# Expert rows summed by accumulating DMAs into four arrays in memory, instead of by the engines after all of them have landed

## The chip, the core and the metric

The kernel runs on one core of a Trainium2 chip. The metric is the device time of one execution, in microseconds; smaller is better. The core has TensorE (PE; its weight loads are PEld), VectorE (DVE), ScalarE (ACT), GpSimd (POOL) and SyncE (SP), and 16 DMA engines that all of them share. In this kernel SP, ACT and POOL issue DMAs.

## What is computed

One transformer layer on 8 sequences of 256 tokens, width 256, all in float32: attention with 16 heads and a distance bias, a layer norm, then a mixture of 32 experts of which each token uses 6, plus a shared expert, and a second layer norm. The part that matters here:

```python
w, idx = _gate(xf, gate_w)                       # 6 of 32 experts per token
g = einsum('td,eid->tei', xf, w11)
u = einsum('td,eid->tei', xf, w33)
act = silu(g) * u
y = einsum('tei,te,edi->td', act, c, w22)        # c: the 6 weights of a token
shared = silu(xf @ sw1.T) * (xf @ sw3.T) @ sw2.T
x = layernorm(x + (y + shared))
```

So each of the 2048 tokens (16 tiles of 128) needs the sum of six rows of 256 floats, one from each of its experts, added to its row of x + shared.

## The kernel before

The program is written out by hand, one instruction stream per engine, with semaphores between them. It has four stages.

**Attention, routing (0 to 310 us).** Eight batches of 256 tokens (`BATCH`), one after the other (`attention_loop`), software-pipelined: while batch b is worked on, PE projects q and k of batch b+1 (`project_q`), ACT and DVE split them into two parts (q_hi, q_lo, k_hi, k_lo), and SP rearranges them through memory (`pack`): four stores to `q_scratch` and `k_scratch`, a wait until all four have landed, then four loads of `q_pack` and two of `k_pack` (L345, L348, L355, L360). PE's scores of batch b+1 (L494) stand in PE's order among the last work of batch b and wait for `qk_packed`. SP works its list in order: in `body(b)` it packs batch b+1, loads, and keeps the normed rows (`keep_x1`). In `body(1)` alone, behind these, it writes the padding rows of the array `routed` (`write_pads`, L383): 8 DMAs of 516 KB from the SBUF tile `empty`, in rows of 1032 bytes. Then comes the loop whose first body packs batch 3. POOL scatters each token's row six times into `routed`, an array in memory with a region for each expert (`dispatch`, L1307, 96 indirect DMAs of 128 rows). Each row carries in its column 256 a code that says where its result belongs, and in column 257 its weight.

**Expert weights and shared expert (310 to 372 us).** 24 DMAs of 512 KB load all expert weights into the SBUF tile `expert_w`.

**The slot loop (372 to 604 us).** The routed rows are worked in `SLOTS` = 128 slots of 128 rows of one expert each. Per slot: SP loads the rows (`xg`, L430), PE turns them (L674), multiplies with w11 and w33 (L682), ACT applies silu (L889), DVE works out the destination rows (`out_row`, L1239) and the product (L1242), PE turns it (L690) and multiplies with w22 (L698), ACT scales into a buffer `ey` (L895), of which there are eight, and POOL sends the 128 result rows of 1 KB with one indirect DMA (`send`, L1320) to `expert_out`, an array with six rows per token. Nothing but its own buffer's readiness (`ey_ready`) holds a send up.

**The last stage (604 to 665 us).** When all sends have landed, SP loads `expert_out` back, one tile of 128 tokens x 6 rows x 1 KB (768 KB) per DMA (`load_y`, L447), into the place of `expert_w`. The tiles are summed in pairs (`pair_loop`): the even tile of a pair by DVE (a reduction L1265 and an add L1270), the odd one by POOL (L1335) and PE (L736, L740, L743, sums in PSUM). Then statistics (L1272, L1276, L1279), an inverse root on ACT and DVE (`polish`), and two applications on ACT (L909), and a store of 256 KB (L913).

Of the kernel before, what the change touches and what calls it, by code (L numbers as in the profile page):

```python
# [50 lines left out]
F_STATS = 7  # L51
# [8 lines left out]
C_ID, C_TRI, C_IOTA, C_SLOT, C_PACK, C_END = 0, 128, 256, 288, 289, 321  # L60
# [46 lines left out]
def build(nc, xT, x, wq, wk, wv, wo, bias, consts, gate_w, expert_weights, sw1, sw3, sw2, out):  # L107
    ctx, early = ExitStack(), ExitStack()
    with ctx:
# [9 lines left out]
        def dram(name, shape, dt=F32):  # L119
# [7 lines left out]
        expert_out = dram("expert_out", [TOKENS * TOPK, DIM])  # L127
# [19 lines left out]
        codes = sb("codes", [P, TILES, TOPK], I32)  # L147
# [70 lines left out]
        expert_w = sb("expert_w", [P, TILES * TOPK * DIM], F32, late)  # L218
# [8 lines left out]
        rows_y = expert_w[:].rearrange("p (t n) -> p t n", t=TILES)  # L227
        f_out = [resid, x1[0]]
        f_resid = x1[1][:]
        y_sum = x1T[0][:, 0, :]  # L230
        y_half = [attn_T[i] for i in range(2)]
        f_bn = sb("f_bn", [P, 2, 2, 6])
        f_mv = sb("f_mv", [P, 2, 2, 2])
        f_small = sb("f_small", [P, 2, 8, 2])
# [39 lines left out]
        y_loaded = [sem(f"y_loaded{i}") for i in range(4)]  # L274
        f_paired = sem("f_paired")
        f_summed, f_stat, f_root, f_fin, f_done = (
            sem("f_summed"), sem("f_stat"), sem("f_root"), sem("f_fin"), sem("f_done"))
# [37 lines left out]

        def pair_loop(eng, body):

            body(0, 0, 0)
            with eng.Fori(0, (TILES // 2 - 2) // 2) as i:
                body(2 * i + 1, 1, i)  # L320
                body(2 * i + 2, 0, i + 1)
            body(TILES // 2 - 1, 1, TILES // 4 - 1)


        @block.sync
        def _(sp):
# [57 lines left out]

            def keep_x1(b, par):
# [4 lines left out]
            def body(b, par, h, one_behind, two_behind, ahead):  # L390
# [48 lines left out]
            for k in range(UNROLL):  # L439
                sp.wait_ge(ey_sent[k], 16 * SLOTS // UNROLL)  # L440
            y_view = expert_out.rearrange("(t p j) d -> t p (j d)", p=P, j=TOPK)

            def load_y(p, par, h):
                for t in range(2):

                    need(sp, y_loaded[2 * par + t], 16 * h)
                    sp.dma_start(rows_y[:, bass.ds(2 * p + t, 1), :].rearrange("p a n -> p (a n)"),  # L447
# [3 lines left out]
            for p in range(2):  # L451
                load_y(p, p, 0)
# [835 lines left out]
        def _(pool):  # L1288
# [36 lines left out]
            with pool.Fori(0, SLOTS // UNROLL) as i:  # L1325
                count = pool.snap(i + 1)
                for k in range(UNROLL):
                    send(k, count)
# [67 lines left out]
```

## Time and profile before

| | |
|---|---|
| median of 3 runs | 668.68 us (667.24 to 672.7) |
| the profiled execution, span of its instructions and DMAs | 665.0 us |
| PE busy | 503.1 us (76%) |
| ACT busy | 345.7 us (52%) |
| DVE busy | 339.3 us (51%) |
| POOL busy | 233.0 us (35%) |
| DMA traffic | 105.33 MB, 62.65 MB read from memory and 42.21 MB written to it |

Spans, rows and sums below are of the profiled execution. An engine's busy time is an average over stages that have different limits, so the stages are read one by one. "Idle before <- X" says how long an engine had nothing to run before an instruction and whose end or landing ended that.

### The profile page before, as it was taken

The numbers are of one execution on the slowest core, as the hardware profiler recorded it, in microseconds if no ns is written. First come the engines' busy times: TensorE is split into PE (matmuls) and PEld (weight loads), VectorE is DVE, ScalarE is ACT, GpSimd is POOL, SyncE is SP. The second block draws the span as 40 slices with busy tenths as digits, with TensorE's granted clock in tenths as the row PEclk, the third lists the DMA queues.
The fourth block names the chain that finished last, engine by engine and source line by source line (L and its number), as shares of the span: only waits on it lengthen the run. The fifth ranks groups of instructions, "written<-read, shape, count | busy, mean of one in ns | idle before, by whom it ended". The sixth has DMA issues, their size and how long they took to land.

```text
span 665.0 us, 12727 instructions
## 1 busy us (share of the span) xinstructions
PE 503.1 (76%) x2773; PEld 384.2 (58%) x2774; DVE 339.3 (51%) x1486; ACT 345.7 (52%) x1085; POOL 233.0 (35%) x256
## 2 busy tenths in 40 slices
PE   3284957395966778586988499999999999993545
PEld 2163745273745556364554378778787787872433
DVE  3143657476674768587454133333333333332986
ACT  1174856485765667584422156556565565661222
POOL 0000000042330606064456045655555555562310
PEclk8597979596986969699889699999999999996776
DMA  6825279638255564524898644454444544415941
GB/s 211 222 58 111 61 179 251 147 98 199 81 135 125 143 158 139 140 92 157 251 301 268 209 121 141 140 146 135 141 143 142 148 137 147 127 48 227 418 175 63
DMA packets 68422, 105.33 MB, mean 158 GB/s; under 512 B 9365, under 2 KB 52890, under 8 KB 68384
## 3 DMA queue, kind: packets, MB, share of 16 engines
q1 hardware_dynamic: 54448, 75.06, 41.2%
q0 software_dynamic: 10752, 25.29, 11.4%
q10 hardware_dynamic: 3184, 4.56, 2.1%
q8 instruction: 13, 0.21, 0.1%
q14 instruction: 25, 0.20, 0.1%
HBM read 62.65 MB, written 42.21 MB: 158 GB/s over the span
## 4 chain that ended last, share of the span: by engine, by line
PE 45%; DMA 31%; SPq 7%; DVE 6%; issue 5%; ACT 4%; POOL 1%; ACTq 1%; DVEq 0%; POOLq 0%
PE bank L682 17%; DMA k_scratch<-k_lo 11%; DMA expert_w<-expert_weights 9%; DMA k_pack<-k_scratch 9%; PE bank L698 8%; PE bank L674 4%; PE bank L508 2%; SPq L355 2%; PE bank L494 2%; PE bank L690 2%; ACT probs L785 2%; PE bank L524 2%; SPq L345 2%; DVE x1T L1265 2%; SPq L383 1%
## 5 line engine op out<-in xcount | busy, mean ns | idle before, releaser
L785 ACT ACTIVATE probs<-s_neg,m_neg 128x128 f32<-128x128 f32 (+1 forms) x256 | 113.8, 447 | 110.3 <-DVE m_neg L967 109.8
L1320 POOL DMA_INDIRECT expert_out<-rows,out_row x128 | 125.9, 984 | 110.2 <-issue 73.4
L682 PE MATMUL bank<-expert_w,xgT 128*128 x512 | 135.9, 388 | 3.7 <-issue 3.6
L1307 POOL DMA_INDIRECT routed<-rows,position x96 | 92.7, 965 | 130.7 <-ACT rows L821 88.1
L967 DVE CUSTOM_DVE_ANT_0 s_neg<-bank,bias_sb 128x128 f32<-128x128 f32 (+1 forms) x256 | 78.9, 354 | 99.9 <-PE bank L494 95.2
L494 PE MATMUL bank<-k_pack,q_pack 128*128 128x256 f32 (+1 forms) x128 | 61.1, 483 | 70.2 <-DMA k_pack<-k_scratch 69.2
L682 PEld LDWEIGHTS bank<-expert_w,xgT 128*128 128x128 f32 x512 | 88.2, 192 | 24.6 <-issue 10.7
L1239 DVE TENSOR_TENSOR out_row<-xg,again 128x1 int32<-128x1 f32 x128 | 21.5, 168 | 147.0 <-ACT eg L889 147.0
L895 ACT ACTIVATE rows<-bank,xg 128x256 f32<-128x256 f32 x128 | 60.7, 474 | 52.1 <-PE bank L698 51.9
L698 PE MATMUL bank<-expert_w,eaT 128*128 x256 | 78.1, 387 | 2.4 <-DVE eaT L1248 1.6
L494 PEld LDWEIGHTS bank<-k_pack,q_pack 128*128 128x128 f32 x128 | 27.9, 221 | 72.6 <-DMA k_pack<-k_scratch 43.1
L889 ACT ACTIVATE eg<-bank 128x128 f32<-128x128 f32 x128 | 35.5, 277 | 40.4 <-PE bank L682 37.9
L674 PE MATMUL bank<-cst,xg 128*128 128x128 f32 x256 | 49.6, 277 | 8.4 <-DMA xg<-routed 8.4
L879 ACT ACTIVATE xgT<-bank 128x256 f32<-128x256 f32 x128 | 48.0, 375 | 13.9 <-PE bank L674 13.8
L524 PE MATMUL bank<-pT,v_sb 128*32 128x128 f32 (+1 forms) x512 | 52.6, 352 | 0.0
L508 PE MATMUL bank<-cst,probs 128*128 128x128 f32 x256 | 46.6, 313 | 5.2 <-ACT probs L785 4.7
L674 PEld LDWEIGHTS bank<-cst,xg 128*128 128x128 f32 x256 | 36.2, 143 | 21.8 <-issue 8.9
L785 ACT ACTIVATION_READ_ACCUMULATOR probs<-s_neg,m_neg 128x1 f32 x256 | 48.3, 189 | 0.0
L508 PEld LDWEIGHTS bank<-cst,probs 128*128 128x128 f32 x256 | 34.8, 159 | 12.5 <-issue 6.5
L524 PEld LDWEIGHTS bank<-pT,v_sb 128*32 128x32 f32 x512 | 28.3, 117 | 23.7 <-issue 9.9
L698 PEld LDWEIGHTS bank<-expert_w,eaT 128*128 128x128 f32 x256 | 38.7, 191 | 5.6 <-issue 4.7
L796 ACT ACTIVATE pT<-bank 128x512 f32<-128x512 f32 x72 | 41.5, 576 | 0.0
(153 smaller groups left out, 729.4 us busy)
## 6 DMA issues: line engine op xcount, KB each, us to landing
xg<-routed SPq DMA_DIRECT2D x128, 129.0 KB, 2.1
expert_w<-expert_weights SPq DMA_DIRECT2D x24, 512.0 KB, 5.3
expert_w<-expert_out SPq DMA_DIRECT2D x16, 768.0 KB, 7.3
q_pack<-q_scratch SPq DMA_DIRECT2D x32, 256.0 KB, 4.4
routed<-empty SPq DMA_DIRECT2D x8, 516.0 KB, 9.1
k_pack<-k_scratch SPq DMA_DIRECT2D x16, 256.0 KB, 6.7
xt<-xT SPq DMA_DIRECT2D x8, 256.0 KB, 6.9
bias_sb<-bias ACTq DMA_DIRECT2D x4, 512.0 KB, 7.6
```

The lines of the kernel that those rows point to most:

```text
L494: pe.matmul(SCORES[u][:, 0:2 * n], q_pack[par][:, 2 * g + pair, P * qb:P * qb + P], k_pack[par][:, g, :, 0:n], start=True, stop=True).then ...
L508: last = pe.transpose(pb[:, at:at + P], probs[g % 2][qb][:, r, 0:P], ident)
L524: last = pe.matmul(O_BANK[at:at + 32, P * kb:SEQ], v_sb[par][:, kb, g, col:col + 32], pT[:, r, :], start=(kb == 0 and r % 2 == 0), stop=(k ...
L674: last = pe.transpose((KV_BANK, Q_BANK)[at % 2][:, P * c:P * c + P], xg[at][:, P * c:P * c + P], ident)
L682: last = pe.matmul(S_BANK[k % 2][:, 0:2 * INTER], xgT[k % 4][:, c, :], w13_sb[:, bass.ds(e, 1), c, :].rearrange("p a n -> p (a n)"), start ...
L698: pe.matmul(DOWN[at % 2][:, 0:DIM], eaT[at % 2][:], w2_sb[:, bass.ds(e, 1), :].rearrange("p a n -> p (a n)"), start=True, stop=True).then_ ...
L785: act.activation(probs[g % 2][qb][:, 2 * pair + r, :], s_neg[u][:, r, 0:n], ACT.Exp, bias=m_neg[:, u, r:r + 1], scale=-1.0, accum_out=row_ ...
L879: act.activation(xgT[at % 4][:].rearrange("p c t -> p (c t)"), (KV_BANK, Q_BANK)[at % 2][:, 0:DIM], ACT.Copy).then_inc(xg_copied[at], 1)
L895: act.activation(ey[at], DOWN[at % 2][:, 0:DIM], ACT.Copy, scale=xg[at][:, DIM + 1:DIM + 2]).then_inc(ey_ready[at], 1)
L967: dve.tensor_tensor_reduce(out=s_neg[u][:, r, 0:n], in0=SCORES[u][:, n * r:n * r + n], in1=bias_sb[:, REP * g + 2 * pair + r, SEQ - n:SEQ] ...
L1307: pool.indirect_dma_start(routed, bass.IndirectOffsetOnAxis(ap=position[:, t, j:j + 1], axis=0), rows[:, t, j, :], None).then_inc(scattere ...
L1320: pool.indirect_dma_start(expert_out, bass.IndirectOffsetOnAxis(ap=out_row[:, k:k + 1], axis=0), ey[k], None, bounds_check=TOKENS * TOPK - ...
```

## The change

The array `expert_out` goes, and four arrays `y_acc` of one row per token (2048, plus 128 rows that nobody reads) come in its place. They are cleared by SP in `body(1)`, right behind the padding rows. `codes` now holds the token's number, the same for its six rows. DVE makes `out_row` with an instruction of two operations: rows that a slot must not send are led to the 128 spare rows. `send` of slot k adds its 128 rows to accumulator k mod 4 by an indirect DMA with an add, and first waits until the send of slot k-4, the one before on this accumulator, has landed. After the loop POOL waits for all sends and issues 16 plain DMAs with an add from the accumulators into `x_sum`, the SBUF tile that already holds x + shared: four tiles of 128 tokens (512 KB) per DMA, the four accumulators of one chunk one after the other, two chunks side by side. DVE then needs only the statistics of `x_sum`, and ACT the application, in chunks of four tiles. PE has no work in the last stage; DVE's and POOL's sums are gone.

```diff
-        expert_out = dram("expert_out", [TOKENS * TOPK, DIM])
+        y_acc = [dram(f"y_acc{n}", [TOKENS + P, DIM]) for n in range(ACCS)]
...
-        codes = sb("codes", [P, TILES, TOPK], I32)
+        codes = sb("codes", [P, TILES], I32)
...
+            def clear_acc(n):
+
+                sp.dma_start(y_acc[n].rearrange("(t p) d -> p t d", p=P),
+                             empty[:, 0:DIM].unsqueeze(1).to_broadcast([P, TILES + 1, DIM])).then_inc(accs_cleared, 16)
...
                 if isinstance(b, int) and b == 1:
                     for i in range(BATCH):
                         write_pads(i)
+                    for n in range(ACCS):
+                        clear_acc(n)
...
-            for p in range(2):
-                load_y(p, p, 0)
-            with sp.Fori(1, TILES // 4) as h:
-                load_y(2 * h, 0, h)
-                load_y(2 * h + 1, 1, h)
...
-            pair_loop(pe, final)
...
+            for c in range(TILES // CHUNK):
+                par = c % 2
+                act.wait_ge(f_stat, FIN_OPS * c + FIN_OPS)
+                act.activation(f_small[:, par, 1, :], f_small[:, par, 0, :], ACT.Ln).then_inc(f_root, 1)
+                act.wait_ge(f_root, 2 * c + 1)
+                act.activation(f_small[:, par, 2, :], f_small[:, par, 1, :], ACT.Exp, scale=-0.5).then_inc(f_root, 1)
+                act.wait_ge(f_fin, 5 * c + 5)
+                if c >= 2:
+                    act.wait_ge(out_stored[par], 16 * (c // 2))
+                for t in range(CHUNK):
+                    act.activation(f_out[par][:, t, :], x_sum[:, CHUNK * c + t, :], ACT.Identity,
+                                   scale=f_small[:, par, 6, t:t + 1], bias=f_small[:, par, 7, t:t + 1]
+                                   ).then_inc(f_done, 1)
+                act.wait_ge(f_done, CHUNK * (c + 1))
+                act.dma_start(out_t[CHUNK * c:CHUNK * c + CHUNK].rearrange("t p d -> p t d"), f_out[par]
...
-                    dve.tensor_tensor(out_row[:, k:k + 1], xg[k][:, DIM:DIM + 1],
-                                      again[:, bass.ds(UNROLL * turn.turn + k, 1)], ALU.add)
+                    dve.tensor_scalar(out_row[:, k:k + 1], xg[k][:, DIM:DIM + 1],
+                                      again[:, bass.ds(UNROLL * turn.turn + k, 1)], trash, ALU.add, ALU.min)
...
+            for c in range(TILES // CHUNK):
+                par = c % 2
+                dve.wait_ge(y_added[c], 16 * ACCS)
+                if c >= 2:
+                    dve.wait_ge(f_done, CHUNK * (c - 1))
+                for t in range(CHUNK):
+                    ins = dve.bn_stats(f_bn[:, t, :], x_sum[:, CHUNK * c + t, :])
+                ins.then_inc(f_stat, 1)
+                dve.wait_ge(f_stat, FIN_OPS * c + 1)
+                for t in range(CHUNK):
+                    ins = dve.bn_aggr(f_mv[:, par, t, :], f_bn[:, t, :])
...
-            def send(k, count):
+            def send(k, count, before):
+
                 need_apart(pool, ey_ready[k], count, passed)
+                if before is not None:
+                    need_apart(pool, ey_sent[(k - ACCS) % UNROLL], before, passed)
                 pool.indirect_dma_start(
-                    expert_out, bass.IndirectOffsetOnAxis(ap=out_row[:, k:k + 1], axis=0),
-                    ey[k], None, bounds_check=TOKENS * TOPK - 1, oob_is_err=False
+                    y_acc[k % ACCS], bass.IndirectOffsetOnAxis(ap=out_row[:, k:k + 1], axis=0),
+                    ey[k], None, bounds_check=TOKENS + P - 1, oob_is_err=True, compute_op=ALU.add
                 ).then_inc(ey_sent[k], 16)
...
+            for k in range(UNROLL):
+                pool.wait_ge(ey_sent[k], 16 * SLOTS // UNROLL)
+            pool.wait_ge(sh_added, TILES)
+            for first in range(0, TILES // CHUNK, 2):
+                for n in range(ACCS):
+                    for c in (first, first + 1):
+                        if n > 0:
+                            pool.wait_ge(y_added[c], 16 * n)
+                        pool.dma_start(x_sum[:, CHUNK * c:CHUNK * c + CHUNK, :],
+                                       y_acc[n][CHUNK * P * c:CHUNK * P * (c + 1)].rearrange("(t p) d -> p t d", p=P),
+                                       accum_op=ALU.add).then_inc(y_added[c], 16)
```

On SP's list, at the end of `body(1)` and the start of the loop (a row is a line of the kernel, what a DMA writes and reads, and its shape; x8 is so many in a row), there stood before:

```order
L387 DMA x_sum<-x_0 128x512
L388 DMA x1T_all<-x1T 128x2x256
L383 DMA routed<-empty 128x4x258 x8
L295 UNCONDITIONAL_BRANCH
L295 ISA
L344 ISA
L345 DMA q_scratch<-q_hi 8x16x512
L348 DMA k_scratch<-k_hi 4x32x256
L345 DMA q_scratch<-q_lo 8x16x512
L348 DMA k_scratch<-k_lo 4x32x256
```

and there stands now:

```order
L382 DMA x_sum<-x_0 128x512
L383 DMA x1T_all<-x1T 128x2x256
L373 DMA routed<-empty 128x4x258 x8
L377 DMA y_acc<-empty 128x17x256 x4
L294 UNCONDITIONAL_BRANCH
L294 ISA
L334 ISA
L335 DMA q_scratch<-q_hi 8x16x512
L338 DMA k_scratch<-k_hi 4x32x256
L335 DMA q_scratch<-q_lo 8x16x512
L338 DMA k_scratch<-k_lo 4x32x256
```

Four clears of 2176 rows of 1 KB stand between the padding rows and the stores of q and k of batch 3; nothing else moved there.

On POOL, the first turn of the slot loop's sends and what follows, with the waits (in brackets), before:

```order
L1325 UNCONDITIONAL_BRANCH
L1325 ISA
L1320 DMA expert_out<-rows,out_row 12288x256 [waits ey_ready0]
L1320 DMA expert_out<-rows,out_row 12288x256 [waits ey_ready1]
L1320 DMA expert_out<-rows,out_row 12288x256 [waits ey_ready2]
L1320 DMA expert_out<-rows,out_row 12288x256 [waits ey_ready3]
L1320 DMA expert_out<-rows,out_row 12288x256 [waits ey_ready4]
L1320 DMA expert_out<-rows,out_row 12288x256 [waits ey_ready5]
```

and now, in the turn that is written out ahead of the loop:

```order
L1273 DMA y_acc<-rows,out_row 2176x256 [waits ey_ready0,accs_cleared]
L1273 DMA y_acc<-rows,out_row 2176x256 [waits ey_ready1]
L1273 DMA y_acc<-rows,out_row 2176x256 [waits ey_ready2]
L1273 DMA y_acc<-rows,out_row 2176x256 [waits ey_ready3]
L1273 DMA y_acc<-rows,out_row 2176x256 [waits ey_sent0,ey_ready4]
L1273 DMA y_acc<-rows,out_row 2176x256 [waits ey_sent1,ey_ready5]
L1273 DMA y_acc<-rows,out_row 2176x256 [waits ey_sent2,ey_ready6]
L1273 DMA y_acc<-rows,out_row 2176x256 [waits ey_sent3,ey_ready7]
```

From the fifth send on each one waits for the landing of the send four places ahead of it as well as for its buffer.

## Rows read from the trace of the kernel before

**Rows 1.** Stages: us, busy of each engine, granted clock, DMA share, GB/s.

```profile
core 0: us, PE busy (x) PEld busy (x) DVE busy (x) ACT busy (x) POOL busy (x), PEclk, DMA share, GB/s
0.00:310.00 310.00, 204.91 (x1382) 156.08 (x1384) 183.77 (x892) 185.91 (x649) 64.16 (x83) 0.83 0.55 140
310.00:372.00 62.00, 49.59 (x161) 28.30 (x159) 31.38 (x115) 15.34 (x19) 32.84 (x38) 0.94 0.87 274
372.00:604.00 232.00, 218.86 (x1154) 178.08 (x1154) 80.07 (x384) 132.75 (x385) 125.89 (x128) 0.98 0.45 130
604.00:665.00 61.00, 29.76 (x78) 21.75 (x78) 44.05 (x96) 11.67 (x32) 10.12 (x8) 0.67 0.61 241
```

**Rows 2.** The chain that ended last, around `body(1)`'s end: start us, us, what.

```profile
96.69 0.62 SPq L383
...
104.81 1.64 SPq L383
...
110.71 9.57 DMA k_scratch<-k_lo
...
122.98 7.13 DMA k_pack<-k_scratch
```

**Rows 3.** Timeline there: PE's next scores and what they waited for.

```profile
130.25 0.57 PE L494 MATMUL bank<-k_pack,q_pack 128*128 128x256 f32 x1 [9.47 <-DMA k_pack<-k_scratch]
```

**Rows 4.** Stages of the padding writes, columns as in rows 1.

```profile
98.00:102.00 4.00, 4.00 (x26) 3.62 (x26) 2.78 (x17) 3.00 (x11) 0.00 (x0) 1.00 1.03 334
102.00:106.00 4.00, 4.00 (x36) 2.94 (x35) 2.82 (x12) 2.64 (x10) 0.00 (x0) 1.00 1.11 277
106.00:110.00 4.00, 3.21 (x28) 2.09 (x27) 3.23 (x20) 3.15 (x12) 0.00 (x0) 1.00 1.15 230
110.00:114.00 4.00, 3.46 (x19) 2.74 (x19) 3.12 (x15) 2.34 (x9) 0.47 (x1) 1.00 1.04 242
98.00:116.00 18.00, 14.67 (x105) 11.40 (x104) 13.68 (x72) 11.67 (x44) 0.47 (x1) 1.00 1.03 261
```

**Rows 5.** POOL's sends in the slot loop, timeline.

```profile
405.39 0.98 POOL L1320 DMA_INDIRECT expert_out<-rows,out_row  x1 [0.64 <-issue]
407.02 0.98 POOL L1320 DMA_INDIRECT expert_out<-rows,out_row  x1 [0.65 <-issue]
...
410.52 0.98 POOL L1320 DMA_INDIRECT expert_out<-rows,out_row  x1 [0.65 <-issue]
412.23 0.98 POOL L1320 DMA_INDIRECT expert_out<-rows,out_row  x1 [0.72 <-issue]
416.13 0.99 POOL L1320 DMA_INDIRECT expert_out<-rows,out_row  x1 [2.92 <-issue]
417.43 0.98 POOL L1320 DMA_INDIRECT expert_out<-rows,out_row  x1 [0.30 <-issue]
```

**Rows 6.** The line L1320: time from issue to landing.

```profile
DMA to landing us min/median/max: 2.1/2.4/4.4
```

**Rows 7.** The chain that ended last, from the last send on.

```profile
602.35 2.09 DMA expert_out<-rows,out_row
604.52 0.37 SPq L447
604.95 5.83 DMA expert_w<-expert_out
...
661.34 1.05 ACT x L909 x2
```

**Rows 8.** Stages of the last part, columns as in rows 1.

```profile
604.00:639.00 35.00, 17.30 (x46) 13.19 (x47) 25.62 (x47) 4.79 (x14) 7.59 (x6) 0.65 0.94 382
639.00:665.00 26.00, 12.47 (x33) 8.56 (x31) 18.43 (x51) 6.88 (x18) 2.53 (x2) 0.70 0.15 50
```

**Rows 9.** Timeline of the end: the small steps of one pair's norm.

```profile
658.24 0.43 DVE L1276 BATCH_NORM_STATS2 f_bn<-bank 128x6 f32<-128x256 f32 x1
658.70 0.25 DVE L1279 BATCH_NORM_AGGREGATE f_mv<-f_bn 128x2 f32<-128x6 f32 x2
659.89 0.20 ACT L920 ACTIVATE f_small<-f_small 128x2 f32<-128x2 f32 x1 [0.47 <-ACT resid L909]
661.34 0.60 ACT L909 ACTIVATE x<-x,f_small 128x256 f32<-128x256 f32 x1 [1.02 <-DVE f_small L1256]
662.42 0.39 ACTq L913 DMA_DIRECT2D out<-x  x1
```

**Rows 10.** DMA issues of 310 to 372 us: KB each, median us to landing.

```profile
expert_w<-expert_weights SPq DMA_DIRECT2D x23, 512.0 KB, 5.3
```

More of the change, by code:

```diff
@@ L50 @@
 GATE_STEPS = 24
-F_STATS = 7
 V_BLANK = 2
@@ L273, in build @@
         ey_ready, ey_sent = sems("ey_ready"), sems("ey_sent")
[L274 to L277, printed above, removed]
+        accs_cleared = sem("accs_cleared")
+        y_added = [sem(f"y_added{c}") for c in range(TILES // CHUNK)]
+        f_stat, f_step, f_root, f_fin, f_done = (
+            sem("f_stat"), sem("f_step"), sem("f_root"), sem("f_fin"), sem("f_done"))
         out_stored = [sem(f"out_stored{i}") for i in range(2)]
@@ L436, in _ @@
                     load_slot(UNROLL * i + k, k, i)
[L439 to L447, printed above, removed]
[L448 to L455 removed]
             for k in range(2):
[L457 removed]
+                sp.wait_ge(out_stored[k], 16 * TILES // CHUNK // 2)
         @block.tensor
@@ L729, in _ @@
             slot_loop(pe, step)
-            def final(p, par, h):
-                need(pe, f_done, 2 * (p - 1))
-                tile = x_sum[:, bass.ds(2 * p + 1, 1), :].rearrange("p a d -> p (a d)")
-                pe.matmul(S_BANK[par][:, 0:DIM], ident, tile, start=True, stop=False)
-                pe.wait_ge(y_loaded[2 * par + 1], 16 * (h + 1))
-                for j in (4, 5):
-                    row = rows_y[:, bass.ds(2 * p + 1, 1), DIM * j:DIM * j + DIM].rearrange("p a d -> p (a d)")
-                    pe.matmul(S_BANK[par][:, 0:DIM], ident, row, start=False, stop=False)
-                pe.wait_ge(f_paired, p + 1)
-                for j in range(2):
-                    last = pe.matmul(S_BANK[par][:, 0:DIM], ident, y_half[par][:, j, :], start=False, stop=(j == 1))
-                last.then_inc(f_summed, 1)
-            pair_loop(pe, final)
         @block.scalar
@@ L1323, in send @@
                 ).then_inc(ey_sent[k], 16)
-            with pool.Fori(0, SLOTS // UNROLL) as i:
-                count = pool.snap(i + 1)
-                for k in range(UNROLL):
-                    send(k, count)
-            def final(p, par, h):
-                pool.wait_ge(y_loaded[2 * par + 1], 16 * (h + 1))
-                need(pool, f_summed, p - 1)
-                row = rows_y[:, bass.ds(2 * p + 1, 1), :].rearrange("p a n -> p (a n)")
-                pool.tensor_tensor(y_half[par][:].rearrange("p c d -> p (c d)"), row[:, 0:2 * DIM],
-                                   row[:, 2 * DIM:4 * DIM], ALU.add).then_inc(f_paired, 1)
@@ L1338, in _ @@
-            pair_loop(pool, final)
+            pool.wait_ge(accs_cleared, 16 * ACCS)
+            for k in range(UNROLL):
+                send(k, 1, 16 if k >= ACCS else None)
+            with pool.Fori(1, SLOTS // UNROLL) as i:
+                count, earlier, now = pool.snap(i + 1), pool.snap(16 * i), pool.snap(16 * (i + 1))
+                for k in range(UNROLL):
+                    send(k, count, now if k >= ACCS else earlier)
+            for k in range(UNROLL):
+                pool.wait_ge(ey_sent[k], 16 * SLOTS // UNROLL)
```

93 lines of the change are left out of this document (25 added, 68 removed).

## The prediction

> **What bounds the kernel now.** I read the stages first, then the chain that ended last inside each of them, then the waits at the places that the change touches. [rows 1] split the span into four. In the first, 310 us long, PE is busy for 205 us and the DMA engines for 55%: neither fills it. The third, the slot loop, takes 232 us of which PE is busy for 219 us at full clock: PE bounds it. There are 128 slots, so a slot takes 232 / 128 = 1.81 us with the loop's start and end, and in its steady part the sends follow each other at 1.6 to 1.7 us [rows 5]. The last stage, 61 us, has no engine full: DVE 44 us, PE 30 us, and the DMA engines only in its first half.
>
> In the first stage the reader is to look at the chain [rows 2]. It runs through SP's eight issues of padding writes, through the store of k_lo that follows them, which lands 9.57 us after its issue, and through a load of k_pack of 7.13 us, and then reaches PE, which has stood idle for 9.47 us for exactly that load [rows 3]. The chain so passes from SP's list straight into PE's wait. This place has no slack: what makes the stores of batch 3 land later makes the scores of batch 3 start later. All PE work that did not need them was done by 121 us, and everything behind the scores is in program order.
>
> **The change, part by part.**
>
> *Clearing.* Four DMAs with 2176 rows of 1 KB each, 8.91 MB, stand in SP's list between the padding writes and the stores of batch 3, on the same queue as both. Their price is the time that the DMA engines need for them, unless the stores overtake. The nearest operation is beside them: the padding writes are the same kind (from the same tile, rows of 1032 bytes, many rows per partition), 4.23 MB. While they run, the DMA engines are full and the rate falls, from 334 over 277 to 230 and 242 GB/s; over the whole of them it is 261 [rows 4]. So the clears take 8.91 / 0.334 = 27 us at best, 8.91 / 0.230 = 39 us at worst, and at the mean 8.91 / 0.261 = 34 us. I take **+34 us**: the low rates come late in a burst, and the clears come last, but rows of exactly 1 KB may go a little better. Nothing hides it. PE already waited for 9.47 us here, so the wait becomes some 43 us. What is late next is all of batch 3; the packing of batch 4 depends on q and k of its own batch, which PE projects inside batch 3, so nothing later catches up. The loads of the expert weights wait for the end of attention and shift with it.
>
> *Sends in the slot loop.* 128 indirect DMAs remain 128 indirect DMAs of 128 rows. Three things are new. (a) Each waits for a second semaphore. Two sends back to back are 0.98 + 0.30 = 1.28 us apart, while on average one is due each 1.6 to 1.7 us [rows 5]; another wait and its increment are a few hundredths to 0.15 us, hidden by that slack of 0.35 us. Behind the waiting send stand only the next sends; a late send is felt first by ACT, which needs its buffer again eight slots later, some 13 us. (b) The landing of the send four places ahead: a send lands 2.4 us after its start in the median, 4.4 us at most [rows 6], and four slots are 6.5 us. With 0.65 us between release and start the chain of an accumulator needs 3.1 us of 6.5, so the add may cost 3.4 us more per send before it holds anybody. Hidden. (c) The instruction itself may take longer, since the add has to read its destination as well: no row shows it. Bounds: 0.98 us as now, or twice that, 1.96 us, if the work grows with the addresses that are written out. I take a value below 1.3 us, up to which PE still bounds the loop, as the one nearest to the only row there is, 0.98 us; this is the weakest step of the sum. **0 us.** DVE's new `out_row` is one instruction for one, on 128 x 1 elements, on an engine that is busy for 80 of 232 us [rows 1]: 0.
>
> *The last send* lands 2.09 us after its start now [rows 7]; with its destination read first I add **+1 us**.
>
> *The last stage.* Before, from the landing at 604.44 us to the end at 665.0 us: 60.6 us, made of a first load and then eight pairs of sums. All of it goes. In its place: 16 DMAs of 512 KB, two chunks side by side, each chunk's four in series, so 8 steps of two. A step's price has two floors. By bytes: plain loads ran at 382 GB/s [rows 8], 1.05 MB in 2.7 us; an add moves its destination through the engine too, so up to 5.5 us. By latency: a load of 512 KB with another one in flight lands 5.3 us after its issue [rows 10], and release to start is 0.65 us [rows 5], so 6 us. Bounds for the eight steps: 8 x 4 = 32 us, if the two chunks overlap well at full rate, and 8 x 8 = 64 us, if doubled bytes and latency add up. I take 6.3 us a step, 50 us, nearest to the latency row with a little for the doubled bytes. Two chunks finish half way and their norms hide behind the other half's transfers. What is left behind the last landing is one chunk's norm: from the last statistics to the application is 661.34 - 658.24 = 3.1 us for one tile [rows 9]; three more statistics of 0.43 us and two more aggregations of 0.13 us make 4.7 us, four applications at about 0.55 us make 2.2 us, and the store from its issue at 662.42 us to the end took 2.6 us for 256 KB, so 3.3 us for 512 KB: 10.2 us. With the first issue, 0.7 + 50 + 10.2 = 61 us instead of 60.6 us: **0 us**, between -18 and +14.
>
> The Trainium skill speaks against this stage (Collectives: The Full Stack, "The bandwidth ceiling: the fold count and why AG ≠ RS ≠ AR"): a transfer that adds reads two sources, and those reads share one ring, so it runs at about half the rate of a copy. No row here shows an adding transfer. By that rule each step would be bound by its bytes at 5.5 us plus an unhidden latency, about 7 us, and the stage would take 67 us, 6 us more than now.
>
> Sum against the profiled execution: 665.0 + 34 + 0 + 1 + 0 = 700 us. The median of the runs is 3.7 us above that span, so **704 us**.
>
> **Rivals.**
>
> *POOL becomes the bound of the slot loop.* For it: the add's extra addresses, and the fact that POOL has just 0.35 us a send to spare, of which the new wait takes a part. Rows 5 also show a send that started 2.92 us late for no releaser, and the following ones back to back: such a stall is caught up only out of this slack. Against it: no row. It decides from an instruction of about 1.3 us on. At 1.5 us with 0.4 us between two, a send takes 1.9 us instead of about 1.7 us: 128 x 0.2 = 26 us, 730 us in all; at 1.96 us, 2.36 us a send, 128 x 0.66 = 84 us, 788 us. PE's busy share in the loop would fall from 94% and its gaps would be ACT's waits for sends. The Trainium skill bears on it (GPSIMD Engine Reference, "4. When to use GPSIMD"): one core of POOL writes the read descriptors and another the write descriptors, so doubled reads would load one of the two; by that the 1.96 us is an upper estimate. Chance 25%.
>
> *The accumulators' chains bind.* A send that adds lands later than 6 us after its start, because the eight or so rows on each DMA engine are read, added and written one by one. For each us beyond, 128 / 4 = 32 turns of a chain cost 32 us: landing at 7 us gives 735 us. Against it: 3.4 us of room, more than a whole plain landing. Chance 10%.
>
> *The clears cost nothing, so that the kernel is not slower.* The DMA engines could take the rows of the stores in between those of the clears, or the scores of batch 3 could have slack after all. Then 665 + 0 + 1 + 3.7 = 670 us: no change; with the last stage at its lower bound too, 652 us. Against it: the same queue carries both, the chain runs through this very place, and PE waits there. It decides only if the clears cost less than some 6 us. Chance 5%, and 2% of it faster.
>
> **How the numbers follow.** The forecast's own mechanism (clears on the path, loop bound by PE) has 60%; its range is 27 to 39 us for the clears and -18 to +14 for the last stage, which are not likely at their ends together: 684 to 722 us. The two rivals that bind in the loop hold 35% and lie from 715 to 790 us; reaching to 750 us leaves out about 12% above, and below 686 us are some 8%. About 1% is what a measurement can tell from no change: faster 2%, within 1% 4%, slower 94%.
>
> **What would show it.** Right: the store of k_lo of batch 3 lands some 34 us later than 120.3 us, PE idles about 43 us ahead of the scores of batch 3, with a rate of 230 to 330 GB/s in between; the slot loop is 232 us long with PE busy for about 219 us; the last stage has two groups of eight transfers with DVE idle in most of it. Wrong: sends longer than 1.3 us with ACT waiting for them; sends that start upon the landing of the one four places ahead; transfers of the last stage far from 6.3 us a step; or an unchanged start of batch 3.

## The result, and the profile after

The changed kernel takes 717.81 us in the median (716.75 to 719.83) beside 670.36 us for the kernel before: a ratio of 1.073, with a 95% interval from 1.068 to 1.078. The profiled execution has a span of 714.9 us, 49.9 us more than before; the medians differ by 47.5 us.

The stages of the changed kernel, in the columns of rows 1:

```profile
0.00:333.00 333.00, 206.86 (x1380) 157.00 (x1381) 183.04 (x890) 186.42 (x649) 64.06 (x82) 0.81 0.57 157
333.00:396.00 63.00, 50.87 (x161) 28.94 (x161) 32.26 (x117) 15.35 (x19) 33.88 (x38) 0.92 0.87 273
396.00:647.00 251.00, 226.63 (x1152) 178.48 (x1152) 86.89 (x384) 132.05 (x385) 199.06 (x128) 0.96 0.84 136
647.00:714.90 67.90, 0.00 (x0) 0.00 (x0) 10.92 (x56) 9.94 (x24) 20.66 (x17) 0.50 0.94 157
```

Three stages have grown, and the second is as it was. What the engines compute is nearly the same up to 647 us: PE's busy time in the first stage is 207 us as before. The growth is waiting. In the slot loop POOL's busy time went from 126 to 199 us with the same 128 sends, and the share of the DMA engines from 0.45 to 0.84. In the last stage the DMA engines are full and the engines nearly empty.

The chain that ended last, at the place of rows 2:

```profile
96.09 0.62 SPq L373
...
107.50 6.78 SPq L377
114.32 5.84 SPq L377
120.20 6.21 SPq L377
126.83 5.28 SPq L335
...
134.84 9.18 DMA k_scratch<-k_lo
...
146.97 6.92 DMA k_pack<-k_scratch
154.03 0.58 PE bank L474
```

The clears (L377) stand in the chain between the padding writes (L373) and the stores, and the scores of batch 3 (L474) start at 154.03 us instead of 130.25 us [rows 3], after a longer wait of PE:

```profile
154.03 0.58 PE L474 MATMUL bank<-k_pack,q_pack 128*128 128x256 f32 x1 [32.13 <-DMA k_pack<-k_scratch]
```

The store of q_hi takes SP 5.28 us to issue where it took 1.05 us, while the clears ahead of it were still running.

POOL in the slot loop, timeline, to be read beside rows 5:

```profile
448.40 1.55 POOL L1273 DMA_INDIRECT y_acc<-rows,out_row  x1 [0.30 <-issue]
450.26 1.55 POOL L1273 DMA_INDIRECT y_acc<-rows,out_row  x1 [0.30 <-issue]
452.12 1.55 POOL L1273 DMA_INDIRECT y_acc<-rows,out_row  x1 [0.30 <-ACT rows L858]
```

A send now takes 1.555 us instead of 0.983 us, and the next one follows after 0.30 us, the least gap that POOL ever had: one send each 1.86 us, with no slack left. Who waited for the sends (us in all, times), and the time from a send's start to its landing:

```profile
  DVE out_row L1196: 40.0, 31
  ACT eg L852: 14.3, 19
...
DMA to landing us min/median/max: 3.8/4.1/5.4
```

A late send is felt first by DVE, which writes `out_row` into the place that the send eight slots earlier reads, and then by ACT. PE, which works on what both make, is busy for 226.6 of this stage's 251 us, 90% instead of 94%.

The chain from the last send on, as in rows 7:

```profile
645.60 3.70 DMA y_acc<-rows,out_row
...
650.02 0.82 POOL x_sum L1294
650.85 8.33 DMA x_sum<-y_acc
659.18 0.28 issue
659.46 6.24 DMA x_sum<-y_acc
...
695.71 6.14 DMA x_sum<-y_acc
...
701.87 1.42 DVE f_bn L1224 x4
...
709.39 2.07 ACT expert_w L878 x4
```

Adding transfers follow each other on landings until 701.84 us, then two chunks are normed one after the other. From these rows and those of before the 49.9 us are divided as follows. The first send starts at 409.24 us instead of 384.92 us: 24.3 us for all that lies ahead of the slot loop. The last send starts at 645.60 us instead of 602.35 us: 18.9 us more, for the loop. It lands after 3.70 us instead of 2.09 us: 1.6 us. From its landing to the end it is 65.6 us instead of 60.6 us: 5.0 us.

### The profile page after: what moved, and what is told of

The parts are those of the page before. It is cut to its first block, busy times and chain, and to the rows that moved or that the text cites. A ratio compares the mean times of both kernels' runs of the same rounds, so it can differ in the third digit from the quotient of the medians.

```text
span 714.9 us, 12389 instructions
## 1 busy us (share of the span) xinstructions
PE 484.4 (68%) x2693; PEld 364.4 (51%) x2694; DVE 313.1 (44%) x1446; ACT 343.8 (48%) x1077; POOL 317.7 (44%) x264
## 4 chain that ended last, share of the span: by engine, by line
DMA 32%; issue 20%; PE 19%; POOL 12%; SPq 10%; ACT 3%; DVE 2%; POOLq 1%; ACTq 1%; DVEq 0%
DMA k_scratch<-k_lo 10%; DMA k_pack<-k_scratch 8%; DMA x_sum<-y_acc 7%; POOL y_acc L1273 6%; POOL routed L1257 6%; PE bank L662 5%; DMA y_acc<-rows,out_row 4%; SPq L377 3%; DMA routed<-rows,position 3%; PE bank L678 2%; PE bank L488 2%; SPq L335 2%; PE bank L474 2%; SPq L345 2%; SPq L373 1%
## 5 line engine op out<-in xcount | busy, mean ns | idle before, releaser
L1273 POOL DMA_INDIRECT y_acc<-rows,out_row x128 | 199.2, 1556 | 56.3 <-issue 36.0
L474 PE MATMUL bank<-k_pack,q_pack 128*128 128x256 f32 (+1 forms) x128 | 62.0, 491 | 91.0 <-DMA k_pack<-k_scratch 90.0
L1196 DVE TENSOR_SCALAR out_row<-xg,again,cst 128x1 int32<-128x1 f32 x128 | 35.0, 273 | 154.4 <-ACT eg L852 113.4
L678 PE MATMUL bank<-expert_w,eaT 128*128 x256 | 80.3, 396 | 4.5 <-DVE eaT L1205 2.6
L474 PEld LDWEIGHTS bank<-k_pack,q_pack 128*128 128x128 f32 x128 | 28.4, 226 | 93.4 <-issue 51.4
L842 ACT ACTIVATE xgT<-bank 128x256 f32<-128x256 f32 x128 | 48.2, 377 | 13.3 <-PE bank L654 13.1
L504 PE MATMUL bank<-pT,v_sb 128*32 128x128 f32 (+1 forms) x512 | 54.3, 360 | 0.0
L1251 POOL COPY rows<-weight 128x12 f32<-128x12 f32 x8 | 2.0, 244 | 111.0 <-DVE weight L1050 111.0
L504 PEld LDWEIGHTS bank<-pT,v_sb 128*32 128x32 f32 x512 | 28.8, 119 | 25.3 <-issue 11.4
```

The costliest lines, as they stand in the source:

```text
L474: pe.matmul(SCORES[u][:, 0:2 * n], q_pack[par][:, 2 * g + pair, P * qb:P * qb + P], k_pack[par][:, g, :, 0:n], start=True, stop=True).then ...
L504: last = pe.matmul(O_BANK[at:at + 32, P * kb:SEQ], v_sb[par][:, kb, g, col:col + 32], pT[:, r, :], start=(kb == 0 and r % 2 == 0), stop=(k ...
L678: pe.matmul(DOWN[at % 2][:, 0:DIM], eaT[at % 2][:], w2_sb[:, bass.ds(e, 1), :].rearrange("p a n -> p (a n)"), start=True, stop=True).then_ ...
L842: act.activation(xgT[at % 4][:].rearrange("p c t -> p (c t)"), (KV_BANK, Q_BANK)[at % 2][:, 0:DIM], ACT.Copy).then_inc(xg_copied[at], 1)
L1273: pool.indirect_dma_start(y_acc[k % ACCS], bass.IndirectOffsetOnAxis(ap=out_row[:, k:k + 1], axis=0), ey[k], None, bounds_check=TOKENS + P ...
```

## Experiments

Each experiment was measured beside its own runs of the kernel before. Beside four of them (half of the rows, the two runs with the clears spread from 128 partitions, and the new last stage) the kernel before itself took 703 to 704 us instead of 670 us. The traces of these four show stalls ahead of one operation of ACT, four in an execution, 37 to 45 us in all and up to 13 us long, and some shorter ones elsewhere, that the other traces don't have; the cause is not known, and the kernel before has no trace in this condition. So these four are compared by ratios or with each other. Where only one execution is given, the times have no interval.

**The clears alone.** To the kernel before, with nothing else changed, the four clears are added:

```diff
                     for i in range(BATCH):
                         write_pads(i)
+                    for n in range(4):
+                        clear_acc(n)
```

> The kernel before with the four clears of the change put in behind the padding writes, on arrays that nothing else uses; all else as before. Theory A (the clears lie on the path, at the rate seen in the changed kernel): the scores of batch 3 start 23.8 us later than in the kernel before, and the time grows by 23 to 25 us, to about 694 us. Rival (part of the changed kernel's delay there came from elsewhere, or later stages take it back): less than 18 us.

Measured: 698.95 us beside 670.45 us, ratio 1.0405 (1.033 to 1.048), 28.5 us. The scores of batch 3 start at 157.71 us, 27.5 us later than before, and the first rows of the slot loop are loaded 31.9 us later, at 404.6 us instead of 372.7 us. So the clears lie on the path, in one piece and by themselves; nothing takes them back. In this execution, the slowest of its four, they cost some us more than in the changed kernel, where the rows of the loop are loaded 24.4 us later. They ran no slower:

```profile
116.00:136.00 20.00, 4.15 (x27) 2.52 (x27) 6.23 (x30) 6.28 (x21) 0.00 (x0) 0.62 1.09 386
```

386 GB/s would be 23 us for 8.91 MB. Some of the rest lies around them: from 100 to 112 us, in the padding writes, the rate was 294, 258 and 236 GB/s instead of 309, 289 and 264 in the changed kernel, and the last store behind the clears landed after 9.98 us instead of 9.18 us. The remainder was not taken apart. This stage scatters: the four executions of this kernel lie between 693.6 and 700.0 us. The expected 23 to 25 us lie in the lower part of the interval, which is 22 to 32 us.

**The clears in rows of 1032 bytes.** The predicted rate came from the padding writes, 261 GB/s, and the clears ran at 376 GB/s (below). The arrays were given 258 columns:

```diff
-        y_acc = [dram(f"y_acc{n}", [TOKENS + P, DIM]) for n in range(4)]
+        y_acc = [dram(f"y_acc{n}", [TOKENS + P, ROW]) for n in range(4)]
```

> The same, but the cleared arrays have rows of 1032 bytes, as the padding writes have: 8.98 MB instead of 8.91 MB. Theory (a row that is no multiple of 256 bytes, and not aligned to one, is what made the padding writes slow, so the prediction's rate was taken from the wrong kind of row): the clears run at about 240 GB/s, 37 us, and the scores of batch 3 start 37 us later than in the kernel before. Rival (the padding writes were slow because of where their rows lie in memory, or because of what else was running): about 24 us, as with rows of 1024 bytes.

Measured: 700.3 us, one execution. The stretch in which only these clears run:

```profile
116.00:142.00 26.00, 4.98 (x27) 2.96 (x27) 6.80 (x32) 6.28 (x21) 0.00 (x0) 0.59 1.09 307
```

Rows of 1032 bytes run at 307 GB/s, rows of 1024 bytes at 386. The row's length is so one part of it, and not the whole: the padding writes, of the same length, fell to 230 GB/s [rows 4]. They go to regions 2.2 MB apart, the clears to one array of 2.2 MB, and other transfers and more work of the engines ran beside them; which of these makes the rest was not separated. Neither theory was right alone. The scores of batch 3 started at 160.91 us; counted from the start of batch 2's, 29.5 us later than before, against 27.9 us with rows of 1024 bytes. The rates differ by 6 us for the whole of the clears, the delays by only 1.6 us, so on the path the row's length is worth less here than the rates say; from one execution of each no more can be told.

**Sends that don't add.** In the changed kernel one word goes:

```diff
-                    ey[k], None, bounds_check=TOKENS + P - 1, oob_is_err=True, compute_op=ALU.add
+                    ey[k], None, bounds_check=TOKENS + P - 1, oob_is_err=True
```

> The changed kernel, but the sends of the slot loop overwrite their rows of the accumulator instead of adding to them (the sums of the expert rows are left out); both waits stay, and so do the clears and the last stage with its additions. Theory A (the add makes POOL's instruction longer, and POOL then bounds the loop): the instruction falls from 1.556 us to 0.98 us, the loop from the first send to the last is 217 to 219 us as before instead of 236 us, and the time falls by 18 to 20 us, to 698 us. Rival B (the instruction is longer for another reason, such as the different bounds check or the wait): it stays at 1.5 us or so, and the time at 717 us.

Measured: 699.29 us, ratio 1.0435 (1.037 to 1.050), 18.5 us below the changed kernel. The line of the sends, duration in ns (least, median, most), first and last start in us:

```profile
L1273 POOL DMA_INDIRECT y_acc<-rows,out_row x128: 982/982/1000, 411.3 to 630.5; - x128
```

And the loop as a stage:

```profile
411.00:631.00 220.00, 211.69 (x1121) 171.40 (x1120) 85.34 (x376) 129.62 (x376) 125.36 (x128) 1.00 0.50 148
```

With both waits in place the sends take 219.2 us from first to last, against 217.4 us in the kernel before and 236.4 us in the changed one, and PE is busy again for 96% of it. So 17.2 of the loop's 18.9 us are the add, as POOL pays for it in each instruction. The other 1.7 us were not traced; among what is left of the change is DVE's new `out_row`, which takes 0.27 us instead of 0.16 us. This run also keeps a difference that the text of the change does not count: the kernel before skips the rows that a slot must not send and moves 12.6 MB with its sends, while now these rows go to the spare rows, and all 16384 rows are sent, 16.65 MB. Sent plainly, they do not lengthen the instruction.

**The waits that don't add.** To the kernel before, the second wait of `send` is given:

```diff
+                if before is not None:
+                    need_apart(pool, ey_sent[(k - 4) % UNROLL], before, passed)
```

> The kernel before, but each send also waits for the landing of the send four places ahead; it still writes plainly to its own rows. Theory A (a plain send lands in 2.4 us, and four slots are 6.5 us): no change, within 1 us, POOL's gap between two sends back to back grows by less than 0.1 us. Rival B (the second wait itself is what pushes POOL to the limit): more than 5 us longer.

Measured: 669.98 us beside 670.45 us, one execution; the sends take 215.7 us from first to last. The waits cost nothing, as predicted.

**Half of the rows.** What in the instruction grows?

```diff
-                    y_acc[k % ACCS], bass.IndirectOffsetOnAxis(ap=out_row[:, k:k + 1], axis=0),
-                    ey[k], None, ...
+                    y_acc[k % ACCS], bass.IndirectOffsetOnAxis(ap=out_row[0:64, k:k + 1], axis=0),
+                    ey[k][0:64], None, ...
```

> The changed kernel, but each send adds only its first 64 rows of 128; the other 64 rows of each slot are left out. Theory A (POOL's instruction has a part that grows with the rows, since it writes out addresses for each, and the add adds to that part): 1.555 us falls to between 0.8 and 1.1 us, and the loop from the first send to the last to the 218 us that PE sets. Rival B (the add's extra 0.57 us is a fixed cost of the instruction): it stays above 1.3 us.

Measured: 732.68 us beside 703.85 us, one execution. The line of the sends, columns as above:

```profile
L1273 POOL DMA_INDIRECT y_acc<-rows,out_row x128: 1397/1402/1475, 439.2 to 660.5; - x128
```

64 rows take 1.402 us, 128 rows 1.555 us. That is 2.4 ns a row; if it is a straight line, 1.25 us are left at no rows at all, more than a whole plain send of 128. Rival B's number held: the instruction stays above 1.3 us, and most of it is fixed. How much of the add's own 0.57 us is fixed depends on whether a plain send of 64 rows is shorter too, which was not measured: between 0.27 us (1.25 - 0.98, if it isn't) and all of it. At 1.402 + 0.30 = 1.70 us a send the loop is 221.3 us long, and the chain that ended last runs through PE in the first part of the loop and through POOL in the rest. So the point from which POOL decides is close to 1.4 us an instruction (217.4 us / 127 sends - 0.30 us = 1.41 us), not 1.3 us as in the prediction.

**Two accumulators.**

```diff
-ACCS = 4
+ACCS = 2
```

> The changed kernel with two accumulators instead of four. The clears are half as long (12 us less), and the last stage has 8 transfers instead of 16 (some 26 us less). Each send waits for the landing of the one two places ahead. Theory A (a send that adds lands 4.1 us after its start and 0.3 to 0.65 us pass from the release to the next start, so a chain of two gives 2.2 to 2.4 us a slot): the loop from the first send to the last takes 280 to 305 us instead of 236 us, and the kernel 725 to 745 us. Rival B (sends in flight together slow each other, and a send alone lands sooner, so that POOL's 1.86 us a send stays the bound): the loop stays at 236 us and the kernel takes about 680 us.

Measured: 746.54 us, one execution, 1.5 us above the range of theory A; 301.6 us from the first send to the last, inside it. POOL now waits for landings:

```profile
500.76 1.55 POOL L1273 DMA_INDIRECT y_acc<-rows,out_row  x1 [1.07 <-DMA y_acc<-rows,out_row]
502.83 1.55 POOL L1273 DMA_INDIRECT y_acc<-rows,out_row  x1 [0.53 <-issue]
505.44 1.55 POOL L1273 DMA_INDIRECT y_acc<-rows,out_row  x1 [1.05 <-DMA y_acc<-rows,out_row]
```

A pair of sends takes 4.7 us: one landing, 3.8 us in the median, and the time from release to start. With four accumulators the same chain has 7.4 us, which four sends of 1.86 us take anyway. The chain is a limit, and four are enough to stay clear of it. The rival fell.

**The last stage without its additions.**

```diff
                                        y_acc[n][CHUNK * P * c:CHUNK * P * (c + 1)].rearrange("(t p) d -> p t d", p=P),
-                                       accum_op=ALU.add).then_inc(y_added[c], 16)
+                                       ).then_inc(y_added[c], 16)
```

> The changed kernel, but the 16 transfers of the last stage copy instead of add (so x + shared and three of four accumulators are left out of the output); their order, sizes and waits stay. Theory A (a row of 1 KB that is added holds a DMA engine for 102 ns instead of 46 ns, and that bounds the stage): the step falls from 6.5 us to between 4 and 5 us, which release, issue and landing then set, and the stage shrinks by 13 to 20 us. Rival B (the stage is bound by the landing that each transfer waits for, not by bytes): less than 6 us.

Measured: 708.15 us, one execution, with a span of 706.3 us. A step takes 5.0 us instead of 6.5 us. From the first transfer at 653.4 us to the end it is 52.9 us instead of 64.9 us in the changed kernel: 12 us less, just under the 13 to 20 us that A expected, and twice what B allowed. The transfers as a stage, of this kernel and then of the changed one:

```profile
654.00:695.00 41.00, 0.00 (x0) 0.00 (x0) 7.12 (x36) 4.97 (x12) 11.46 (x16) 0.50 0.76 230
```

```profile
650.00:702.00 52.00, 0.00 (x0) 0.00 (x0) 5.59 (x29) 4.97 (x12) 20.51 (x16) 0.50 1.09 173
```

Adding, the DMA engines are full at 173 GB/s, the stores of the output included; copying the same bytes, they are busy for 76% and landings set the pace. The queue of these transfers alone, again of this kernel and then of the changed one (packets, MB, and their time as a share of the 16 engines' stretch):

```profile
q0 software_dynamic: 2298, 8.39, 68.5%
```

```profile
q0 software_dynamic: 8017, 7.96, 102.7%
```

Copying, that is 8.39 MB in 68.5% of 41 us, 299 GB/s of busy time; adding, 7.96 MB in 102.7% of 52 us, 149 GB/s, half of it. The additions also go in packets of 1 KB where the copies go in longer ones. How much the packets' size adds to the price was not separated; the clears, writes in packets of 1 KB, ran at 386 GB/s. POOL's instruction also falls from 1.27 to 0.75 us. So the stage is bound by the time that the DMA engines need for the additions.

**The clears spread out.** SP waits some 9 us in each batch for the next q. In place of the block, a quarter of each accumulator is cleared in each of four bodies, first from 32 partitions:

```diff
+                if not isinstance(b, int):
+                    clear_part(b)
...
+                    part = y_acc[n][bass.ds(n_rows * (b - 2), n_rows), :].rearrange("(p t) d -> p t d", t=TILES + 1)
+                    sp.dma_start(part, empty[0:32, 0:DIM].unsqueeze(1).to_broadcast([32, TILES + 1, DIM])
```

> The changed kernel, but the clears are spread: a quarter of each accumulator (four DMAs of 544 KB) behind the keeping of the rows in each of the bodies of batches 2 to 5, where SP waits some 9 us for the next q. Theory A (the clears cost their time only because they stand on the path in one block of 24 us): the scores of batch 3 start as in the kernel before, at about 130 us, most of the 24 us come back, and the time is 697 to 702 us. Rival B (the 8.9 MB cost the same wherever they stand, because the stores and loads of q and k wait for the DMA engines in every batch): 715 us or more.

Measured: 716.98 us, ratio 1.071 (1.062 to 1.080): nothing gained. The scores of batch 3 start at 129.88 us, as before, but those of batches 4 to 7 start 6, 11, 18 and 26 us later than in the kernel before: each batch adds 5 to 8 us. One stage of them shows why:

```profile
136.00:146.00 10.00, 9.75 (x78) 8.01 (x74) 6.90 (x36) 7.98 (x28) 5.41 (x6) 1.00 0.87 200
```

From 32 partitions the clears run at 200 GB/s, other traffic included, so that a quarter takes 11 us and runs into the stores. The time is what rival B expected, but a clear that is too slow for the gap would give it under theory A too, so both were left standing, and a second version writes from all 128 partitions:

```diff
+                    part = y_acc[n][bass.ds(TOKENS // 4 * (b - 2), TOKENS // 4), :].rearrange("(t p) d -> p t d", p=P)
+                    sp.dma_start(part, empty[:, 0:DIM].unsqueeze(1).to_broadcast([P, 4, DIM])
```

> The changed kernel with its clears spread over the bodies of batches 2 to 5 again, but written from 128 partitions in rows that alternate between partitions, as in the block, not from 32 partitions; the 128 spare rows of each accumulator are cleared in body 1. In the first spread version the clears ran at 185 GB/s, 11 to 12 us for each quarter, and ran over the 9 us in which SP waits anyway. Theory A (only the part beyond that gap costs): each quarter takes 5.6 us at 375 GB/s, fits, and the time falls to 695 to 703 us. Rival B (the DMA engines' time is taken from the stores and loads of every batch, fit or not): 712 us or more.

> The kernel of the run before this one with clears spread from 128 partitions, once more, beside fresh runs of the kernel before: in that run the kernel before itself took 704 us instead of 670 us, with small steps of DVE and ACT between the batches taking longer, so what the spread clears hide behind may differ. Theory A (each quarter fits into SP's gap of 9 us): where the kernel before takes 670 us, this one takes 695 to 703 us, a ratio of 1.037 to 1.049, and the first rows of the slot loop are loaded within 3 us of the kernel before. Rival B (they were hidden only behind the slower steps there): 708 us or more.

Measured: 721.85 us beside 703.85 us, ratio 1.025 (1.020 to 1.029), and once more 723.87 us beside 703.19 us, 1.030 (1.027 to 1.032). In both the kernel before was slow, so the times expected can't be compared. What can be is the trace of the half-row kernel, which was measured beside the same runs and has the block of clears and the same work up to the slot loop: it starts the scores of batch 3 at 156.98 us and loads the first rows of the loop at 426.9 us; with the clears spread these are 129.99 us and 401.6 us, 25.3 us earlier (129.57 us and 404.5 us in the second run, 22.4 us earlier). The half-row kernel and the first of the two have nearly the same stalls of ACT, 37 and 38 us in all. So in these traces spreading takes the clears off the path, as far as one trace of the block can show it; the changed kernel itself has no time in this condition. Whether spreading gains as much where the kernel before takes 670 us stays open: that is where theory A and rival B differ, and neither run shows it.

**The padding writes spread, and the last stage of before.** The same thought, on the kernel before:

```diff
-                if isinstance(b, int) and b == 1:
-                    for i in range(BATCH):
-                        write_pads(i)
+                if not isinstance(b, int):
+                    for i in range(2):
+                        write_pads(2 * (b - 2) + i)
```

> The kernel before, but its eight padding writes are spread, two behind the keeping of the rows in each of the bodies of batches 2 to 5, instead of eight in one block. If blocks of writes ahead of the stores of q and k are what costs (theory A), the wait of PE ahead of the scores of batch 3, 9.5 us, shrinks by 5 to 8 us and the time falls by as much, to about 662 us, 1% faster than the kernel before. Rival B (each pair of padding writes delays the batch that it stands before by its own 4 us): no change or slower by up to 8 us.

Measured: 665.91 us beside 670.27 us, ratio 0.995 (0.9915 to 0.9988): 4.4 us in the medians, less than the 5 to 8 us expected. PE's wait ahead of batch 3 falls from 9.47 to 2.67 us, as expected, and a part comes back: batch 4 starts 6.0 us earlier than in the kernel before, batch 7 only 1.4 us. On top of that, the last stage:

```diff
-                need(pe, f_done, 2 * (p - 1))
+                need(pe, f_done, 2 * (p - 3))
...
+                pool.tensor_tensor(rows_y[:, 2 * p, 2 * DIM:4 * DIM], rows_y[:, 2 * p, 0:2 * DIM],
+                                   rows_y[:, 2 * p, 2 * DIM:4 * DIM], ALU.add).then_inc(f_evened, 1)
```

> The kernel before with the padding writes spread, as in the run on these, and its last stage changed: POOL adds rows 0 and 1 of each even tile into its rows 2 and 3, so that DVE's reduction takes four rows instead of six, the eight pairs are written out, and PE's sums use four banks in turn instead of two, so that PE can run ahead of ACT. Theory A (the stage of the kernel before is bound by a cycle of DVE's reduction, ACT's application and PE's sums of 6.3 us a pair, not by its loads, which are done 35 us into it): the pair falls to about 5 us, the stage by 6 to 12 us, and the time to 654 to 660 us. Rival B (the loads set the pace): less than 3 us.

Measured: 692.28 us beside 703.85 us, ratio 0.983 (0.979 to 0.986), the lowest ratio of all kernels here; its stage from the first load to the end is 56.5 us instead of 60.5 us in the trace of the kernel before. That is 4.0 us, between the 6 to 12 us of theory A and the less than 3 us of rival B. With the 4.4 us of the padding writes it makes 8.4 of the 11.6 us gained; the rest is not explained. While the loads run, a pair takes 5.6 to 7.6 us, about as before; behind them it takes 4.6 us. So neither theory holds alone. From the chain that ended last in this part, of which DVE's reductions (L1264) are still the largest piece:

```profile
658.88 1.93 DVE x1T L1264
...
661.81 1.12 DVE f_small L1020
...
675.29 1.90 DVE x1T L1264
...
679.88 1.90 DVE x1T L1264
```

## Why the prediction was right, and where it was not

The sign and the range held: 717.8 us lie in 686 to 750 us and 14 us above the 704 us predicted. The mechanism held for the clears, and not for the slot loop, which PE was to bound and POOL bounds. That the time came so near is luck in part: 10 us too much for the clears hide half of the 19 us that were put at nothing for the loop. The steps one by one:

- *The path runs through SP's list into the scores of batch 3.* Right. PE idles there for 32.13 us instead of 9.47 us, and with the clears alone for 35.62 us.
- *The clears cost 34 us, at 261 GB/s.* The term was too large: 24.3 us. The mean rate of the padding writes was carried over to rows of another length at other addresses. The stretch with the clears alone:

```profile
114.00:134.00 20.00, 4.97 (x27) 2.95 (x27) 6.97 (x33) 6.28 (x21) 0.00 (x0) 0.54 1.07 376
```

  8.91 MB at 376 GB/s are 23.7 us. The upper end of the range of rates, 334 GB/s, should have been higher: the loads of the last stage, 382 GB/s [rows 8], were a row of a full DMA queue too.
- *The add makes the send no longer than 1.3 us, so the loop costs 0.* This step failed, and the prediction called it its weakest. It chose the only row there was, of a plain send. The instruction takes 1.555 us, POOL became the bound, and the loop grew by 18.9 us, 17.2 of them by the add alone. The first rival, with 25%, had this mechanism; it put the point from which POOL decides at 1.3 us, where it is about 1.4 us, and at 1.5 us it priced 26 us, since it put 0.4 us between two sends where 0.30 us are seen. It looked for the late sends in ACT's waits; DVE's `out_row` waits for them first, 40.0 us against ACT's 14.3 us. The half-row run shows that at least about half of the extra time does not grow with the rows, so the work is not simply doubled. The Trainium skill (GPSIMD Engine Reference, "4. When to use GPSIMD") says that one core of POOL writes the read descriptors and another the write descriptors; no run here shows the two apart.
- *The second wait is hidden; the chain of four is hidden.* Right, both: 669.98 us with the waits alone, and the landing of 4.1 us in the median leaves a chain of four with room.
- *The last send +1 us.* 1.6 us.
- *The last stage costs 0, between -18 and +14.* 5.0 us. The eight steps took 51.8 us, 6.5 us each, against 6.3 us; right, though by luck in part: it was put together from a landing of 5.3 us and 0.65 us from release to start, with a little for the bytes. Measured are 6.2 us in the median and 0.28 us, and the DMA engines' time for the additions decides. The Trainium skill (Collectives: The Full Stack, "The bandwidth ceiling: the fold count and why AG ≠ RS ≠ AR") says that adding needs two source reads on one ring and so runs at about half the rate of a copy. The trace agrees, with 149 GB/s of busy time against 299 GB/s. The 67 us that the prediction estimated by this rule were nearer to the 65.6 us measured than the forecast's 61 us, but not for the steps: 56 us by the rule, 50 us in the forecast, 51.8 us measured. The tail behind the last landing took 13.1 us, not 10.2 us, since both chunks land together and the second one waits for DVE and ACT.

So two terms were off by 10 and by 19 us with opposite signs, the last stage by 5 us, and the time came out 14 us above the forecast.

## What to carry to other kernels

An add that moves from an engine into the DMAs is paid in three currencies: the issuing engine's instruction, the DMA engines' time, and clearing what is added to. Before making such a change, measure one adding transfer; here 0.57 us more in each of 128 sends used up a slack of some 0.4 us that no busy share showed. And look where the clears go: here a block of writes ahead of small stores that an engine waits for cost its whole length, 24 us of it. Try to put them where the queue's owner waits anyway, at full rate; in the traces here that took them off the path, though its gain in the kernel's time is not shown. And take a rate from rows of the same length and place.

## What the hardware showed

- A send of 128 rows of 1 KB with an add takes POOL 1.555 us instead of 0.983 us, and 1.402 us with 64 rows. It lands in 4.1 us instead of 2.4 us in the median.
- With adding sends the DMA engines are busy for 84% of the slot loop at 136 GB/s; with the same rows sent plainly, for 50% at 148 GB/s. Per byte the sends' own queue is busy 2.8 times as long (16.65 MB in 61.0% of 238 us against 23.3% of 220 us), more than the factor of two in the last stage.
- Adding transfers of 512 KB, two in flight, ran at 173 GB/s with the DMA engines full, the output's stores included; the same transfers copying at 230 GB/s with them at 76%.
- Writes from SBUF to memory: 386 GB/s in rows of 1024 bytes, 307 GB/s in rows of 1032 bytes, down to 230 GB/s where these go to regions 2.2 MB apart beside other transfers, 200 GB/s from 32 partitions, other traffic included.
- DVE on a tile of 128 x 2 elements took 1.11 us where it takes 0.16 us otherwise, just while POOL ran its addition of 128 x 512 elements (two rows of the timeline of the kernel with the new last stage):

```profile
661.62 1.29 POOL L1332 TENSOR_TENSOR expert_w<-expert_w 128x512 f32<-128x512 f32 x1 [0.66 <-DMA expert_w<-expert_out]
661.81 1.11 DVE L1020 TENSOR_TENSOR f_small<-f_small 128x2 f32<-128x2 f32 x1
```
